# Gated cross-attention and mixture-of-experts layer: each indirect scatter of the first three batches waits for the landing of the scatter ahead of it

## The reference

```python
x = x + tanh(g_xattn) * attention(layernorm(x), ctx, ctx)     # 16 heads of 16
z = layernorm(x)
shared = swiglu(z @ sw1 + sb1) @ sw2 + sb2                    # one shared expert
probs  = softmax(z @ gate_w + gate_b)                         # 8 routed experts
cw     = probs where among the two largest of a token, else 0
routed = sum over e of cw[e] * (swiglu(z @ rw1[e] + rb1[e]) @ rw2[e] + rb2[e])
out    = x + tanh(g_ffn) * (shared + routed)
```

## Time and profile before

| | us |
|---|---|
| time of three runs, median (lowest to highest) | 741.25 (738.51 to 744.33) |
| the profiled execution: its own time | 741.77 |
| the profiled execution: span of the core | 740.0 |
| busy: PE, DVE, ACT, POOL | 647.2, 501.3, 426.1, 242.4 |
| first scatter starts on POOL | 533.79 |
| first tile's load is issued by SP | 602.01 |
| last accumulating DMA of a tile starts on POOL | 726.97 |

### The profile page before, as it was taken

The page is one execution under the profiler, slowest core; times in us unless marked ns, Lnnn a source line. Parts: engine busy times, 40 slices in busy tenths (PEclk is TensorE's granted clock), DMA queues, the critical chain, the costliest instruction groups (busy, mean ns, idle before and its releaser), DMA issues.

```text
span 740.0 us, 12662 instructions
## 1 busy us (share of the span) xinstructions
PE 647.2 (87%) x3616; PEld 338.5 (46%) x3616; DVE 501.3 (68%) x829; ACT 426.1 (58%) x842; POOL 242.4 (33%) x240
## 2 busy tenths in 40 slices
PE   3788677879999999999999999978886969999990
PEld 3677451223233323333333332344364758888880
DVE  5799889748888888888888888547536734433430
ACT  3665244647777777777777777745523214544440
POOL 8342224033422443134000122100175503545542
PEclk9899897979999999999999999999987989999995
DMA  8879687925696687977566340010029994665545
GB/s 276 285 223 317 194 211 169 162 47 102 108 218 181 185 175 142 202 194 166 77 100 85 60 85 1 20 39 0 9 107 356 418 277 95 96 97 94 85 46 138
DMA packets 82858, 108.11 MB, mean 146 GB/s; under 512 B 16528, under 2 KB 64570, under 8 KB 81853
## 3 DMA queue, kind: packets, MB, share of 16 engines
q1 hardware_dynamic: 72080, 78.88, 45.7%
q0 software_dynamic: 10736, 28.71, 15.0%
HBM read 62.10 MB, written 47.35 MB: 148 GB/s over the span
## 4 chain that ended last, share of the span: by engine, by line
PE 66%; issue 14%; DVE 7%; POOL 5%; DMA 3%; another core or an unknown queue 2%; SPq 1%; POOLq 1%; ACT 0%; DVEq 0%; ACTq 0%
PE psO L1464 16%; PE psS L1437 16%; PE psM L1419 13%; PE psH L1682 7%; POOL parts L581 3%; PE psY L1708 3%; PE psX L1532 2%; PE psH L1638 1%; PE psH L1679 1%; PE psX L1670 1%; PE psH L1693 1%; DMA acc<-ysb,ids 1%; PE psO L1507 1%; PE psM L1437 1%
## 5 line engine op out<-in xcount | busy, mean ns | idle before, releaser
L810 ACT ACTIVATE pr<-psS 128x512 f32<-128x512 f32 x488 | 266.6, 595 | 109.2 <-PE psS L1437 109.0
L1073 DVE TENSOR_REDUCE mneg<-psM 128x1 f32<-128x1024 f32 x240 | 282.6, 1220 | 68.6 <-PE psM L1419 68.5
L1437 PE MATMUL psS<-qst,kst 99*128 99x512 bf16 x488 | 153.8, 388 | 12.1 <-DMA qst<-msb 11.5
L1464 PE MATMUL psO<-pr,vt 128*32 128x512 f32 x1024 | 138.3, 612 | 0.0
L1419 PE MATMUL psM<-kst,qst 96*128 96x512 bf16 x480 | 127.4, 386 | 6.4 <-DVE mneg L1073 4.1
L1437 PEld LDWEIGHTS psS<-qst,kst 99*128 99x128 bf16 x488 | 39.9, 97 | 160.5 <-ACT pr L810 129.9
L720 POOL DMA_INDIRECT acc<-ysb,ids x39 | 60.2, 1543 | 74.7 <-ACT ysb L933 43.9
L1419 PEld LDWEIGHTS psM<-kst,qst 96*128 96x128 bf16 x480 | 46.3, 98 | 65.5 <-DVE mneg L1073 10.6
L567 POOL TENSOR_TENSOR msb<-mcp,none 16x128 bf16<-16x128 f32 x16 | 6.2, 389 | 209.1 <-ACT mcp L787 209.0
L1682 PE MATMUL psH<-wall,zgT 128*128 x234 | 70.3, 437 | 0.0
L1308 DVE TENSOR_TENSOR rg<-psH,rs 128x256 f32<-128x256 f32 x39 | 16.6, 424 | 68.5 <-ACT rs L921 65.1
(11 more groups left out here) (244 smaller groups left out, 869.0 us busy)
## 6 DMA issues: line engine op xcount, KB each, us to landing
kst<-k_parts SPq DMA_DIRECT2D x96, 128.0 KB, 5.8
w_parts<-wraw POOLq DMA_DIRECT2D x14, 768.0 KB, 4.7
wall<-w_parts SPq DMA_DIRECT2D x7, 1536.0 KB
v_pad<-vst SPq DMA_DIRECT2D x16, 512.0 KB, 7.6
vt<-v_pad SPq DMA_DIRECT2D x16, 512.0 KB, 7.6
wraw<-wexp POOLq DMA_DIRECT2D x9, 768.0 KB, 6.7
k_parts<-parts SPq DMA_DIRECT2D x16, 384.0 KB, 6.1
qst<-q_parts SPq DMA_DIRECT2D x96, 64.0 KB, 5.3
```

Of the source, the lines that this page charges most:

```text
L810: nc.scalar.activation(pr[:, slot, j], score_bank(s, j), ACT.Exp, scale=SCALE).then_inc(e_done, 1)
L1073: V.tensor_reduce(mneg[:, parity, i:i + 1], psM[:, i % 2], X_AXIS, ALU.max, negate=True).then_inc(m_free, 1)
L1437: mm(score_bank(s, j), kst[:, slot, j, kt * P:(kt + 1) * P], qst[:, slot, j], start=True, stop=True).then_inc(s_full, 1)
L1464: last = mm(psO[j * VW:(j + 1) * VW, u % 2], vt[:, u, k, j * VW:(j + 1) * VW], pr[:, k % 4, j], start=(k == 0), stop=(k == KT - 1), skip_g ...
```

## The change

One wait is added in front of the scatters of batches 0, 1 and 2. `n` is the scatter's number in that order, from 0 to 23. Scatter `n` waits until `sc_done` has reached 16 times `n`, which is when all scatters ahead of it have landed. The first one has no such wait, and the eight of batch 3 have none. Nothing else is changed, and no instruction is moved.

```diff
                 pool.wait_ge(sl_ok, b + 1)
                 for k in range(2):
                     for t in range(QT):
+                        n = 2 * QT * b + k * QT + t
+                        if 0 < n < 2 * QT * (NB - 1):
+
+                            pool.wait_ge(sc_done, 16 * n)
                         nc.gpsimd.indirect_dma_start(
                             out=zs[:, :],
                             out_offset=bass.IndirectOffsetOnAxis(ap=slot_u[:, b, k * QT + t:k * QT + t + 1], axis=0),
```

## The result

The changed kernel takes **790.74 us** (median of 4 runs, 789.20 to 792.42) against 740.78 for the kernel before (4 runs), a ratio of 1.0678 with a 95% interval of 1.0645 to 1.0711. The forecast was 785.5, in a range of 770 to 804. The profiled execution of the changed kernel has a span of 790.2 us, 50.2 more than before.

What follows compares the result with a forecast made beforehand. POOL's scatters were taken to decide when 11 MB of weights move; the waits delay the first tile's load by 44.7 us. Span 740.0 + 44.5 = 784.5, plus 1.8 outside, 786.3, or 785.5 for a median run; range 770 to 804.

Steps and rivals of the forecast that it cites:

- The wait on free wires: Batches 0 and 1: each step grows from 1.28 to 3.3 us, 30.2 us for 15 waits, all on the path.
- The conversion from the accumulating DMA: Scatter step from an accumulating DMA's 4.66 us, less 0.57 for the instruction and 0.8 for packets: 3.3 us.
- Rival 2: Plain scatter's landing lags its instruction's end by 2.3 us, like the accumulating DMA's: step 4.1, time 802.5; chance 0.16.
- Who is behind POOL: Behind batches 0 and 1: L689 (new L693) moves from 555.27 to 585.5, SP's weight loads to 586.3.
- The first step of batch 2: Batch 2's first scatter queues behind L691's 1 MB of zeros under full wires: 14.5 us for the step.
- The six steps behind it: Rest of batch 2, sharing engines with weight packets: four steps of 4.7 and two of 3.8, 26.4 us.
- What is late next: After batch 2: POOL's 12.09 idle gone, SP waits 14 us for `brow_ok`, first tile's load at 646.7, +44.7.
- The sum: Whole kernel: span 740.0 + 44.5 = 784.5, 1.8 more outside it, 786.3 profiled, 785.5 for a median run.
- Rival 1: Only the first 30 us count; batch 2 doesn't queue behind the megabyte, steps 3.3 each: 771.5 us; chance 0.12.
- Rival 3: No slower: scatters land within 1.28 us of their start, so waits are free: 738.5 us; chance 0.02.

Runs made afterwards that it cites:

- batches 0 and 1 alone: Changed kernel in the control's form, with waits on scatters 1 to 15 only, none in batch 2: 770.22 us, 1.042 against the kernel before.
- two in flight: Changed kernel in the control's form, each scatter waiting for the one before the last, on two semaphores in turn: 754.04 us, 1.019 against the kernel before.
- the control: Kernel before, with POOL's 39 wait counts in the routed stage bounded at run time, two short instructions more for each: 740.1 us, 1.0007.
- the block moved, no waits: The control with POOL's block (zeros, b2_sh, megabyte to acc, constants) moved ahead of scatter(0), no added waits: 728.03 us against 740.55, 0.9826.

## Why the prediction was right, and where it was off

**The wait on free wires: right.** Forecast 3.3 us a step and 30.2 for fifteen waits; measured 3.31 and 49.64 - 19.28 = 30.4. The conversion from the accumulating DMA held: 2.43 to 2.72 from start to landing, ten of the fifteen at 2.43 to 2.45, and 0.8 from landing to the next start. Rival 2, 4.1 a step, is refuted: a plain scatter lands 1.5 us behind its instruction's end, not 2.3. The Trainium skill's rule of about 2.0 us plus bytes by 436 GB/s ("DMA: Bandwidth & Descriptors", "Anatomy of one DMA — SWDGE (gpsimd) path") gives an estimate of 2.3; it is near the 2.44 if it is counted from the start of the instruction, and not if it is counted from the end, as I had weighed it. That most of it is the receipt of the write, this trace does not bear out: the scatter of 538.82 has its last packet in 540.9 to 541.0 and lands at 541.29.

**Who is behind POOL: right.** L693 came at 586.80, forecast 585.5; this execution's scatters also began 1.7 later than those of the profile before. The kernel with batches 0 and 1 alone shows that this part costs 31.5 by itself.

**The first step of batch 2: right in kind, 2.4 short.** Forecast 14.5, measured 16.88. With SP's packets four times smaller it is 8.6, and with no weights beside it 5.45, so it is the megabyte of zeros that alternates with the weights. The 2.4 us are in the megabyte's end: I had it through at 601.0 in the times of this execution (14.2 behind L693), and it lands 16.7 behind its issue at 587.16, at 603.9. The scatter behind it lands 1.7 later, as forecast.

**The six steps behind it: the step that was mis-sized.** I had "a step of 3.3 + 1.4 = 4.7" under full wires and 26.4 us for six; measured were 7.74, 7.17, 6.40 and three of 3.25, 31.1. Two errors partly cancel in that sum: a step beside the weights is 7 us and not 4.7, but only three of the six met full wires and not four, and the free ones are 3.25 and not 3.8. I took the price of sharing from a queue that was never empty. There the scatters' 3 packets for each engine pass in 1.5 us. A scatter that is issued into an empty queue of its own beside the weights has its first packet 3 us behind its instruction's end in place of 0.5, which a queue with a backlog hides, and its packets then take 2.6 us and not the 1.9 of the forecast. That two in flight take 7.6 us together shows that the wait is a delay and not a rate, and that packets of 3 KB don't shorten it shows that it isn't so many packets of the other queue. Its cause stays open.

**What is late next: right.** POOL's 12.09 of idle was used up, SP waited for `brow_ok` (26.6 us, forecast 14), PE's and DVE's delay in the shared expert was hidden in PE's 47.44 us of idle. From the last scatter of batch 2 to the tile's load: 16.70, forecast 17.7. Of that, 0.56 is the very last scatter, 0.98 us in place of 1.54, and 0.34 the way from L508 to L524, where SP's issues are shorter on free wires (0.30 in place of 0.47 in the first of them). The 12.09 belong in part to the one-off delay of the profile before: in the control POOL's idle there is 3.89, while SP comes to L508 10.4 us behind POOL's memset and not 5.6.

**The sum.** 654.13 - 602.01 = 52.12 is 1.69 of a later start, 30.36 for the fifteen waits, -0.52 between the parts, and 20.59 for batch 2 and what follows (forecast 14.5). The routed experts are 1.9 shorter, but the waits did little of that, since the control has 136.4 without any. It goes with PE's pause ahead of the first tile. After pauses of 5.07 us (profile before) and 4.5 (the block moved, no waits) PE comes to the tiles at 2.4 GHz (granted clock 1.00), falls to 1.2 GHz (0.50) as it begins, and is at 2.4 GHz again 9.6 and 9.0 us behind the load; the stage takes 138.0 both times. After pauses of 13.39 (control) and 47.44 (changed kernel) the clock is at 0.50 already when the load is issued, and it rises 6.0 and 6.5 us behind it; the stage takes 136.4 and 136.1. Forecast +44.5 for the span, measured +50.2. The later start and the shorter stage nearly cancel, by luck; the miss is batch 2's.

**Rival 1** (only the first 30 count) is refuted: it had batch 2's steps at 3.3 each. The kernel without batch 2's waits took 770.2 and the rival's figure was 771.5, because both leave SP's own work as what ends last. **Rival 3** is refuted by the first step.

## What to carry to other kernels

A wait for the landing ahead costs its whole latency each time, and three terms decide what it is: the instruction, the way to the landing, and the restart of the waiting engine; here 1.0, 1.5 and 0.8 us. Ask what stands behind the waiting engine in program order: here one memset behind 16 scatters released 11 MB of loads, and moving it ahead of them was worth 12.5 us in the kernel before. Beside loads that fill the wires, a transfer that is issued alone waits far longer than the same one in a backlog, so price it from a lone one; two in flight took back 36.5 of the 50 us. And look at a second profile before a stage's end is taken for a floor: the 8.61 us in which DVE stood still were in one execution and not in the control's.

## What the runs showed of the hardware that I had not expected

A scatter of 139 KB, alone in its queue beside loads that fill the 16 engines, has its first packet 3.0 us (12 KB packets beside it) or 3.2 us (3 KB packets) after its instruction ends, 0.5 on free wires, and 1.2 to 1.6 beside writes in packets of 0.5 KB that fill the engines as well. What holds it, the fetching of its descriptors or reads already in flight, no run here tells apart; it stays open. Of the arbitration, the Trainium skill ("DMA: Bandwidth & Descriptors", "Queues, rings and completion order") says that an engine takes the queues in turn, packet by packet. The backlog agrees (251 packets against 246 in 8 us), and so, roughly, does the megabyte of zeros beside small packets (259 against 228 in 4 us, though 81 against 44 in the first of them); the 3 us come on top.
